# An LSTM layer of 1024 steps with a modulated linear layer: the forget gate summed first, the cell by one scan, tanh by a sigmoid

## The reference

```python
xW = x @ Wx + b                        # (2, 1024, 1024), gates i, f, o, g of 256 each
h, c = cond, 0
for t in range(1024):
    a = xW[:, t] + h @ Wh
    i, f, o, g = sigmoid(a_i), sigmoid(a_f), sigmoid(a_o), tanh(a_g)
    c = f * c + i * g
    h = o * tanh(c)
    hs[:, t] = h
x = x + hs
ys = cond / sqrt(256)
d = rsqrt((ys * ys) @ (w * w) + 1e-8)
x = x + ((x * ys) @ w) * d
```

## Time and profile before

| what | value |
|---|---|
| median of 3 runs | 1866.57 us (1865.84 to 1866.58) |
| the profiled execution, whole | 1865.51 us |
| its span, first to last instruction | 1863.7 us |
| TensorE busy (modelled) | 1794.8 us, 96% |
| VectorE busy | 916.5 us, 49% |
| ScalarE busy | 900.9 us, 48% |
| GpSimd busy | 259.2 us, 14% |
| mean granted TensorE clock | 0.994 |

### The profile page before, as it was taken

How to read it: one execution, slowest core, us unless ns; L and a number is a source line. 1 busy time by engine, 2 the same in 40 slices (tenths; PEclk the granted TensorE clock), 3 DMA queues, 4 the chain that set the end, 5 groups by cost and what they waited for, 6 DMA issues and landing times.

```text
span 1863.7 us, 358217 instructions
## 1 busy us (share of the span) xinstructions
PE 1794.8 (96%) x165116; PEld 1627.1 (87%) x165116; DVE 916.5 (49%) x11034; ACT 900.9 (48%) x6148; POOL 259.2 (14%) x1293
## 2 busy tenths in 40 slices
PE   7999999999999999999999999999999999999998
PEld 6888888888888888888888888888888888888886
DVE  2454544455445544454444544455444544455444
ACT  2444444444444444444444444444444444444443
POOL 0111111111111111111111111111111111111110
PEclk7999999999999999999999999999999999999999
DMA  3000000000000000000000000000000000000001
GB/s 98 0 0 0 0 0 0 0 0 0 0 0 0 0 0 0 0 0 0 0 0 0 0 0 0 0 0 0 0 0 0 0 0 0 0 0 0 0 0 45
DMA packets 4585, 6.69 MB, mean 4 GB/s; under 512 B 1248, under 2 KB 3040, under 8 KB 4576
## 3 DMA queue, kind: packets, MB, share of 16 engines
q1 hardware_dynamic: 3872, 5.51, 0.9%
q10 hardware_dynamic: 704, 1.05, 0.2%
HBM read 4.46 MB, written 2.10 MB: 4 GB/s over the span
## 4 chain that ended last, share of the span: by engine, by line
PE 85%; DVE 10%; ACT 3%; issue 2%; DMA 0%; SPq 0%; POOL 0%; DVEq 0%
PE pG L209 51%; PE pX L191 17%; PE pS L209 12%; DVE junk L340 6%; PE pF L222 3%; ACT gates L176 3%; DVE hst L351 2%; DVE pG L322 1%; PE pX L290 1%; DVE gates L340 0%; DMA xh<-in_xT_dram 0%; PE pS L281 0%; DVE ores L368 0%; SPq L105 0%; ACT tanhc L182 0%
## 5 line engine op out<-in xcount | busy, mean ns | idle before, releaser
L209 PEld LDWEIGHTS pG<-hst,wh_sb 128*32 128x32 f32 x98304 | 981.1, 111 | 219.1 <-DVE hst L351 172.1
L209 PE MATMUL pG<-hst,wh_sb 128*32 128x16 f32 x98304 | 1081.8, 186 | 60.6 <-DVE hst L351 53.4
L340 DVE CUSTOM_DVE_ANT_1 junk<-gates 128x4 f32<-128x4 f32 x4096 | 506.9, 162 | 824.7 <-ACT gates L176 772.5
L176 ACT ACTIVATE gates<-pG 128x6 f32<-128x6 f32 x2048 | 372.5, 182 | 928.7 <-PE pG L209 782.9
L209 PE MATMUL pS<-hst,wh_sb 128*32 128x16 f32 x32768 | 495.5, 185 | 0.0
L191 PE MATMUL pX<-xp,wx_sb 128*32 128x8 f32 x32896 | 459.3, 181 | 2.8 <-issue 1.8
L137 POOL TENSOR_TENSOR xh<-xh,hst 128x4 f32 (+1 forms) x1024 | 208.6, 204 | 1575.4 <-DVE hst L351 1575.4
L182 ACT ACTIVATE tanhc<-gates 128x2 f32<-128x2 f32 x2048 | 410.5, 200 | 13.5
L209 PEld LDWEIGHTS pS<-hst,wh_sb 128*32 128x32 f32 x32768 | 397.9, 108 | 0.0
L191 PEld LDWEIGHTS pX<-xp,wx_sb 128*32 128x32 f32 x32896 | 391.8, 108 | 3.2 <-issue 1.9
L351 DVE TENSOR_TENSOR hst<-tanhc,ogate 128x2 f32<-128x2 f32 x2048 | 329.7, 161 | 100.4 <-ACT tanhc L182 0.2
(11 more groups left out here) (30 smaller groups left out, 13.9 us busy)
## 6 DMA issues: line engine op xcount, KB each, us to landing
outT_dram<-ores SPq DMA_DIRECT2D x8, 256.0 KB, 2.5
xh<-in_xT_dram SPq DMA_DIRECT2D x6, 320.0 KB
wh_sb<-in_Wh_dram ACTq DMA_DIRECT2D x1, 1024.0 KB, 8.0
wx_sb<-in_Wx_dram SPq DMA_DIRECT2D x1, 1024.0 KB, 7.4
w_sb<-in_w_dram SPq DMA_DIRECT2D x1, 256.0 KB, 6.9
xh<-in_xT_dram SPq DMA_DIRECT2D x2, 64.0 KB, 7.9
condT<-in_condT_dram ACTq DMA_DIRECT2D x1, 2.0 KB, 7.7
bias_col<-in_bC_dram ACTq DMA_DIRECT2D x1, 3.0 KB, 7.4
```

What stands on the lines that cost most here:

```text
L176: act.activation(gates[:, j, :, 0:NG].rearrange("p b n -> p n b"), cells[j][:, :, cols], ACT.Sigmoid).then_inc(gates_ready[j], 1)
L209: last = pe.matmul(to[c * Q:(c + 1) * Q, :], tile(wh_sb[:, k, :], c, j, g), hst[:, k, WIDE * t:WIDE * (t + 1)], start=False, stop=True, sk ...
L340: cell = dve.tensor_tensor_reduce(out=junk[:, j, b, :], in0=gates[:, j, b, AT_I:AT_F + 1].unsqueeze(2).broadcast_to([P, 2, 2]), in1=gates[ ...
```

## The change

- PSUM: i and g of a half stay in a bank of `pG` (`pairs`); f gets a bank of its own per half (`pH`, `forgets`). `pX` shrinks from three banks to one. The second layer sums in `pG`'s banks in place of `pX`'s.
- TensorE: after the wait for half 1 of h the order is f, i, g for half 0, then for half 1 g (k = 0), f (both k), i, g; f has its own semaphore, `fsum_ready`. 32 passes stand ahead of the wait in place of 36. Step 3 has no filler.
- ScalarE: f by itself, then i and g by one instruction (4 columns). Then per half the cell's activation first and the output gate second; the cell's activation is a sigmoid with scale 4, and `factors_ready` is given by the output gate behind it.
- VectorE: f * c by a `tensor_tensor`; then, after a wait for it and for ScalarE's i and g, one `tensor_tensor_scan` over six elements per half. Its recurrence is state = a * state + b, three steps for each sequence: 0 * state + G, then 1 * state - 0.5, then i * state + f * c, and the third is the new cell (at half its value, as before). The write of h becomes (sigmoid - 0.5) * o by a `scalar_tensor_tensor`: h is stored halved.
- Since h is halved, `wh_sb` is doubled for i, f, o and taken times 4 for g; GpSimd first doubles h into `whole`, waits for that, then adds it to x.
- The carries are split: a pair and a forget carry per half, and the one for o.

```diff
-    FILL = (0, 0, 1, 1)
+    FILL = (0, 0, 1, 0)
...
+        whole = sb("whole", [P, T, K, B])
+        parts = sb("parts", [P, K, 2 * B * SCAN])
+        fgate = sb("fgate", [P, K, B])
+        cellc = sb("cellc", [P, K, B * SCAN])
...
+        pH = ctx.enter_context(nc.psum_tensor("pH", [P, K, 512], F32))
+        pX = ctx.enter_context(nc.psum_tensor("pX", [P, 512], F32))
+        pairs = [pG[:, j, 0:2 * WIDE].rearrange("p (n r) -> p n r", r=WIDE) for j in range(K)]
+        forgets = [pH[:, j, 0:WIDE] for j in range(K)]
+        cells = [[pairs[j][:, 0, :], forgets[j], pairs[j][:, 1, :]] for j in range(K)]
...
-                        pool.tensor_tensor(now, now, hst[:, :, at:at + B].unsqueeze(3), ALU.add).then_inc(xh_ready, 1)
+                        pool.tensor_tensor(whole[:, s, :, :], hst[:, :, at:at + B], hst[:, :, at:at + B], ALU.add).then_inc(whole_ready, 1)
+                        pool.wait_ge(whole_ready, it * T + (s + 1))
+                        pool.tensor_tensor(now, now, whole[:, s, :, :].unsqueeze(3), ALU.add).then_inc(xh_ready, 1)
...
                     for j in range(K):
+                        act.wait_ge(fsum_ready[j], it * T + (s + 1))
+                        act.activation(fgate[:, j, :], forgets[j][:, cols], ACT.Sigmoid).then_inc(fgate_ready[j], 1)
                         act.wait_ge(sums_ready[j], it * T + (s + 1))
-                        act.activation(gates[:, j, :, 0:NG].rearrange("p b n -> p n b"), cells[j][:, :, cols],
-                                       ACT.Sigmoid).then_inc(gates_ready[j], 1)
+                        act.activation(parts[:, j, SCAN - 1:SCAN - 1 + 8].rearrange("p (n q) -> p n q", n=2)[:, :, ::SCAN],
+                                       pairs[j][:, :, cols], ACT.Sigmoid).then_inc(parts_ready[j], 1)
                     for j in range(K):
+                        act.wait_ge(cell_ready[j], it * T + (s + 1))
+                        act.activation(sigc[:, j, :], cellc[:, j, SCAN - 1::SCAN], ACT.Sigmoid, scale=4.0)
                         act.wait_ge(osum_ready[j], it * T + (s + 1))
-                        act.activation(ogate[:, j, :], outs[j][:, cols], ACT.Sigmoid)
-                        act.wait_ge(cell_ready[j], it * T + (s + 1))
-                        act.activation(tanhc[:, j, :], gates[:, j, :, AT_C], ACT.Tanh, scale=2.0).then_inc(tanh_ready[j], 1)
+                        act.activation(ogate[:, j, :], outs[j][:, cols], ACT.Sigmoid).then_inc(factors_ready[j], 1)
...
                     pe.wait_ge(h_ready[0], it * T + (s + 1))
-                    for n in range(NG):
-                        cell(s, 0, n, 0)
+                    cell(s, 0, 0, 0)
+                    cell(s, 0, 2, 0)
...
+                    cell(s, 0, 1, 0)
...
                     cell(s, 1, 0, 0)
-                    cell(s, 1, 1, 0, early)
 
                     pe.wait_ge(h_ready[1], it * T + (s + 1))
-                    for n in range(NG):
-                        last = cell(s, 0, n, 1)
-                    last.then_inc(sums_ready[0], 1)
-                    cell(s, 1, 1, 0, late)
+                    cell(s, 0, 1, 1).then_inc(fsum_ready[0], 1)
+                    cell(s, 0, 0, 1)
+                    cell(s, 0, 2, 1).then_inc(sums_ready[0], 1)
                     cell(s, 1, 2, 0)
-                    for n in range(NG):
-                        last = cell(s, 1, n, 1)
-                    last.then_inc(sums_ready[1], 1)
...
+                    cell(s, 1, 1, 0)
+                    cell(s, 1, 1, 1).then_inc(fsum_ready[1], 1)
+                    cell(s, 1, 0, 1)
+                    cell(s, 1, 2, 1).then_inc(sums_ready[1], 1)
...
-            dve.tensor_scalar(wh_sb[:, :, g_cols], wh_sb[:, :, g_cols], 2.0, None, ALU.mult).then_inc(operands_ready, 1)
+            ifo_cols = slice(0, (O_ + 1) * D)
+            dve.tensor_scalar(wh_sb[:, :, ifo_cols], wh_sb[:, :, ifo_cols], 2.0, None, ALU.mult)
+            dve.tensor_scalar(wh_sb[:, :, g_cols], wh_sb[:, :, g_cols], 4.0, None, ALU.mult).then_inc(operands_ready, 1)
...
                     for j in range(K):
-                        dve.wait_ge(gates_ready[j], it * T + (s + 1))
-                        for b in range(B):
-                            cell = dve.tensor_tensor_reduce(
...
+                        dve.wait_ge(fgate_ready[j], it * T + (s + 1))
+                        dve.tensor_tensor(parts[:, j, (B + 1) * SCAN - 1::SCAN], fgate[:, j, :], cellc[:, j, SCAN - 1::SCAN],
+                                          ALU.mult).then_inc(parts_ready[j], 1)
+                        if s == T - 1 and j == 1:
+                            carry_pair(0)
+                        dve.wait_ge(parts_ready[j], it * (2 * T) + 2 * (s + 1))
+                        dve.tensor_tensor_scan(cellc[:, j, :], parts[:, j, 0:B * SCAN], parts[:, j, B * SCAN:2 * B * SCAN], 0.0,
+                                               ALU.mult, ALU.add).then_inc(cell_ready[j], 1)
...
+                        dve.wait_ge(factors_ready[j], it * T + (s + 1))
+                        at = h_slot((s + 1) % T)
+                        dve.scalar_tensor_tensor(out=hst[:, j, at:at + B], in0=sigc[:, j, :], scalar=-0.5, in1=ogate[:, j, :],
+                                                 op0=ALU.add, op1=ALU.mult).then_inc(h_ready[j], 1)
                         if s == T - 1 and j == 0:
-                            carry_cells(1)
+                            carry_forget(0)
+                            carry_pair(1)
                     if s == T - 1:
+                        carry_forget(1)
                         carry_outs()
```

More of the change, by code:

```diff
@@ L81, in build @@
         osum_ready = [sem(f"osum_ready{j}") for j in range(K)]
-        gates_ready = [sem(f"gates_ready{j}") for j in range(K)]
-        bias_doubled = sem("bias_doubled")
-        x_carried = [sem(f"x_carried{n}") for n in range(K + 1)]
+        fsum_ready = [sem(f"fsum_ready{j}") for j in range(K)]
+        fgate_ready = [sem(f"fgate_ready{j}") for j in range(K)]
+        parts_ready = [sem(f"parts_ready{j}") for j in range(K)]
+        bias_doubled, whole_ready = sem("bias_doubled"), sem("whole_ready")
+        pair_carried = [sem(f"pair_carried{j}") for j in range(K)]
+        forget_carried = [sem(f"forget_carried{j}") for j in range(K)]
+        outs_carried = sem("outs_carried")
         cell_ready = [sem(f"cell_ready{j}") for j in range(K)]
-        tanh_ready = [sem(f"tanh_ready{j}") for j in range(K)]
+        factors_ready = [sem(f"factors_ready{j}") for j in range(K)]
         h_ready = [sem(f"h_ready{j}") for j in range(K)]
@@ L236, in _ @@
             pe.wait_ge(operands_ready, 3)
-            pe.wait_ge(x_carried[0], 1)
-            early, late = range(G // 2), range(G // 2, G)
+            pe.wait_ge(pair_carried[0], 1)
             with pe.Fori(0, NBODY) as it:
@@ L299, in _ @@
             dve.memset(picks[0:1, 0:1], 1.0).then_inc(operands_ready, 1)
-            dve.memset(gates[:, :, :, :], 0.0).then_inc(buffers_zeroed, 1)
+            dve.memset(parts[:, :, :], 0.0).then_inc(buffers_zeroed, 1)
+            dve.memset(cellc[:, :, :], 0.0).then_inc(buffers_zeroed, 1)
             dve.memset(hst[:, :, :], 0.0).then_inc(buffers_zeroed, 1)
-            dve.wait_ge(buffers_zeroed, 2)
-            dve.memset(gates[:, :, :, AT_HALF:AT_HALF + 1], -0.5)
+            dve.wait_ge(buffers_zeroed, 3)
+            dve.memset(parts[:, :, 1:B * SCAN:SCAN], 1.0)
+            dve.memset(parts[:, :, B * SCAN + 1::SCAN], -0.5)
             dve.wait_ge(cond_loaded, 16)
@@ L316, in _, with carry_pair, carry_forget @@
             dve.wait_ge(wh_loaded, 16)
[L317 removed]
+            ifo_cols = slice(0, (O_ + 1) * D)
+            dve.tensor_scalar(wh_sb[:, :, ifo_cols], wh_sb[:, :, ifo_cols], 2.0, None, ALU.mult)
+            dve.tensor_scalar(wh_sb[:, :, g_cols], wh_sb[:, :, g_cols], 4.0, None, ALU.mult).then_inc(operands_ready, 1)
             for j in range(K):
[L319 to L323, removed]
+                dve.tensor_scalar(hst[:, j, h_slot(0):h_slot(0) + B], condT[:, j, :], 0.5, None, ALU.mult).then_inc(h_ready[j], 1)
+            def carry_pair(j):
+                dve.tensor_tensor(pairs[j][:, :, 0:ROWS], xcells[j][:, ::2, :], bias_col[:, j, ::2].unsqueeze(2).broadcast_to([P, 2, ROWS]),
+                                  ALU.add).then_inc(pair_carried[j], 1)
+            def carry_forget(j):
+                dve.tensor_tensor(forgets[j][:, 0:ROWS], xcells[j][:, 1, :], bias_col[:, j, 1:2].broadcast_to([P, ROWS]),
+                                  ALU.add).then_inc(forget_carried[j], 1)
             def carry_outs():
                 dve.tensor_tensor(pS[:, :, 0:ROWS], xouts, bias_o[:, :].unsqueeze(2).broadcast_to([P, K, ROWS]),
[L327 removed]
+                                  ALU.add).then_inc(outs_carried, 1)
             dve.wait_ge(bias_doubled, 1)
@@ L345, in _ @@
-                        cell.then_inc(cell_ready[j], 1)
-                        if s == T - 1 and j == 0:
```

(10 more changed lines are left out.)

34 lines of the change are left out of this document (18 added, 16 removed).

## The result

The changed kernel takes 1915.56 us (median, 1914.48 to 1916.73) against 1866.21 us of the kernel before beside it: ratio 1.0266, interval 1.0253 to 1.0279, so 49 us slower. Forecast were 1892 us, 26 us more than before, and a range of 1848 to 1940: the sign and the mechanism came as said, the loss was forecast at half its size.

What follows compares the result with a forecast made beforehand. The prediction took h0's cycle to bind the kernel before and h1's the changed one: its thirteen terms give 1.794 against 1.769 us, +0.025 a step, x 1024 = +25.6 us. Forecast 1892 us, range 1848 to 1940.

Steps and rivals of the forecast that it cites:

- h1's cycle: From the end of h1's write to its next end: 1.73 us before, 1.79 after, ruling the changed kernel's step.
- f x c late: VectorE's product before the scan: ready at 1.13 by way of f, against 1.08 by the (i, g) leg.
- ogate behind the cell's sigmoid: On ScalarE ogate follows the 0.20 sigmoid by 0.10 and ends 0.27 after its start: +0.07 on h1's cycle.
- own wait: On VectorE the scan waits for f x c on its own engine: 0.03 us.
- thirteen terms: The steps of h1's cycle in the changed kernel, from h1 to its next write: sum 1.79 us, unrounded 1.794.
- rival A: The f path is covered and the (i, g) leg ends last: 1.74 us a step, 1836 to 1862 us; 20%.
- h0's cycle before: In the kernel before, h0's write to its next: 1.77 us, binding, since tanh 0 stands behind ogate 0.
- the five carries: Five carries in place of three per four steps: nothing in the steps; two more at the start add 0.2 us.
- B: The scan on VectorE costs what it replaces, 0.25: 1.87 us a step, about 1970 us; 9%.
- C: GpSimd holds VectorE where their instructions overlap: +0.02 to +0.06 us a step on top, 1910 to 1950 us; 12%.
- D: With less fill TensorE's granted clock might fall to 1.2 GHz: over 2300 us if always; 1%.
- E: Over the whole kernel, gains and losses cancel within 0.2%; 5%.

Runs made afterwards that it cites:

- e1: Changed kernel with the product f * c and its wait left out (output wrong): 1884.73 us, ratio 1.0087 to the kernel before.
- e5: Changed kernel with f of half 1 summed 32 passes ahead of g in place of 16: 1884.06 us, ratio 1.0091 to the kernel before.
- e3: Changed kernel with ScalarE's order cell's sigmoid 0, ogate 0, ogate 1, cell's sigmoid 1: 1858.09 us, ratio 0.9940 to the kernel before.
- e7: Kernel before with only tanh of the cell put ahead of the output gate in each half: 1914.69 us, ratio 1.0254.
- e2: Changed kernel with the output gate again ahead of the cell's sigmoid in each half: 1909.9 us, ratio 1.0214 to the kernel before.

## Why the prediction was right, and where it was short

**Mechanism: right, and shown.** The forecast had h1's cycle rule in place of h0's, with f x c late by 0.05 (0.03 to 0.04 in the trace, and e1 and e5 each win 0.03) and ogate behind the cell's sigmoid as +0.07 (e3 wins 0.06; e7 loses 0.03 by it, since h1 had 0.04 to spare in the kernel before). It had h1 0.36 behind h0 (0.37), TensorE standing for 0.08 before h1 (0.10), the own wait of 0.03, the sigmoid from SBUF at 0.20, the write of h at 0.16 and the scan at 0.17.

**Size: short by 0.03 us a step, and TensorE's leg was the term.** The sum of thirteen terms gave 1.79; the same terms in the trace, as medians over the steps, give 1.823:

| term, us | predicted | measured |
|---|---|---|
| h1 to first pass | 0.060 | 0.056 |
| 48 passes to the end of f1 | 0.427 | 0.436 |
| pass to fgate | 0.250 | 0.271 |
| fgate and handover | 0.200 | 0.204 |
| f x c and own wait | 0.190 | 0.195 |
| scan and handover | 0.200 | 0.204 |
| cell's sigmoid to ogate | 0.100 | 0.110 |
| ogate, handover | 0.200 | 0.186 |
| write of h | 0.160 | 0.161 |
| sum | 1.787 | 1.823 |

The first three rows are TensorE's leg, from h1 to the reader of f1's sum: 0.763 where the sum had 0.737. That is 0.026 of the 0.036; the other rows, up and down, come to 0.010 together, of which rounding explains 0.007 (unrounded, the prediction's sum is 1.794). The step that failed is therefore the price of this leg. It was taken from the kernel before, as 8.9 ns a pass and 0.25 behind the last one, and did not hold for sums that are cut and signalled otherwise. The same shows in rival A's leg to the (i, g) activation of half 1: 0.06 + 0.57 + 0.24 = 0.87 in the prediction, 0.921 in e5.

What the price hangs on can be read from the distances at which TensorE signals one sum behind the other. They are the same to 0.001 us in every run, and since each reader starts 0.022 to 0.024 behind its signal, ScalarE's lines show them too:

| passes in the sum | distance of the signals, us | for instance |
|---|---|---|
| 8 | 0.092 | e5, 903.93 to 904.02 |
| 16 | 0.159 | changed kernel, 905.40 to 905.56 |
| 24 | 0.226 | changed kernel, 905.56 to 905.78 |
| 32 | 0.292 | e5, 904.02 to 904.32 |
| 36 | 0.326 | kernel before, 902.02 to 902.35 |

All five lie on one line: 8.3 ns a pass and 0.025 us for each sum that is signalled, whichever bank it is in. The changed kernel signals six sums a step in place of four, the two of f by themselves; by this line that is 0.05 more on the way to output sum 0, which two of them precede. e2, with the same passes, measured 0.036 there. No run leaves a signal out with all else kept, so that the signal itself, and not something else at the end of a sum, takes the 0.025 is argued and not shown.

**h0's cycle before: as predicted.** The prediction says ogate 0 waited for output sum 0. It starts 0.16 behind the second gates activation, which could also be a spacing that ScalarE keeps between two activations from PSUM. It is not: in e5 one follows another by 0.09 (903.93 to 904.02). The 0.16 is the distance of two sums of TensorE of 16 passes each. In the changed kernel ogate 0 was off the path as said, but by 0.01 in place of 0.04, since output sum 0 too came later.

**What lay beside:** the five carries, the scaled weights and the filler cost nothing visible (1.5 us of the 49 are outside the loop's 48). A gain on the other side had been overlooked: in the kernel before, the first step of a body is late by 0.12 in 57 of 256 bodies (7 us in all); in the changed kernel TensorE's late passes there, 0.03, fall into the stand before h1. The ordinary steps lost 0.053 (1.770 to 1.823), where 0.025 was forecast.

**The rivals.** A (f covered, the (i, g) leg ends last) was no case of the changed kernel; e5 makes it true, and even then the step is 1.79, above the 1.74 that A gave it, by the 0.05 of TensorE's leg (0.921 against 0.87). B fell with the scan's 0.17. C was a real mechanism in the wrong place: a hold shows only in the six bodies in which GpSimd has its long instructions, where the scan beside them took three times as long. In the step above GpSimd's 0.20 from 905.55 ends before f x c 0 does (905.60 and 0.16) and costs it nothing. GpSimd and then VectorE of the changed kernel:

```profile
129.34 0.61 POOL L155 TENSOR_TENSOR wsq<-w_sb 128x256 f32<-128x256 f32 x1
```

```profile
129.43 0.55 DVE L370 TENSOR_TENSOR_SCAN cellc<-parts 128x6 f32<-128x6 f32 x1
```

That is 0.28 us in each of the six, under 2 us in all. D and E did not occur.

## What to carry to other kernels

In a recurrence spread over four engines, write down for each half of the state the whole cycle from its write to its next write, before and after, with the position of each instruction in its engine's queue: the share of the busiest engine on the profile's page (TensorE, 83%) names neither of the two waits that e1 and e3 price. An instruction that is moved off one engine so as to be "free" is free only if its leg ends before the other leg; here it was late by 0.03 us, and summing its operand 16 passes earlier paid for it. The order of two activations can be right for the first half of a vector and wrong for the second, and that order alone decided between 1.027 and 0.994. And where the difference asked for (0.025) is a tenth of a term (0.25), do not carry that term over from another grouping of the sums: take what one more signalled sum costs from the distances of the sums that the trace has (here 36 passes in 0.33, 16 in 0.16).

## What the runs showed of the hardware

- TensorE's sums in this kernel come 8.3 ns a pass and 0.025 us a signalled sum apart (8 passes 0.092, 16 passes 0.159, 24 passes 0.226, 32 passes 0.292, 36 passes 0.326), in all runs alike.
- How closely two short ScalarE activations follow each other, start to start, where neither waits for another engine: one from PSUM behind one from SBUF 0.09 to 0.11 us (904.35 to 904.44 in e1, 906.39 to 906.50), one from SBUF behind one from PSUM 0.07 (903.04 to 903.11, 903.30 to 903.37). Two from PSUM were 0.09 apart at the least (e5), and there the second still waited for its sum; so their own distance is not known, only that it is no more.
- An instruction of VectorE that ran beside a long one of GpSimd, with no semaphore between the two, took 0.38 us beyond its 0.17, from 129.43 to 129.98, where GpSimd's ended at 129.95: it ended with GpSimd's and not by its own length.
- At the start of a loop body TensorE's passes can come late, though h is there: 0.96 in place of 0.83 us for 96 passes in e7, in nearly every body, 0.12 us in one body of four or five in the kernel before, 0.07 in nearly every body of e2. In e7 the first nine passes are on time and the tenth starts 0.07 late. No wait stands there (that for a carry comes ahead of pass 25), so it is neither h nor a carry. The branch lies just ahead of the body; whether it is that, or the wait for GpSimd at the end of the body, was not tried.
